# First attention of a two-layer perceiver: context channels split as 128 and 64 rows, and one PSUM set for keys and one for values

## What is computed

```python
xn = layernorm(x, ln_x_g, ln_x_b)            # x: context, 64 x 257 x 192
ln = layernorm(latents, ln_l_g, ln_l_b)      # 64 x 32 x 256
q = ln @ Wq.T
kv = jnp.concatenate([xn @ Wkv.T, ln @ Wlkv.T], axis=1)
k, v = (kv[..., :INNER], kv[..., INNER:])    # INNER 256 = 4 heads x 64
qn = rmsnorm(q, qn_g) * SCALE
kn = rmsnorm(k, kn_g)
attn = softmax(where(mask, qn @ kn.T, -max)) # 289 keys per head
out = (attn @ v) @ Wo.T + bo
```

## Time and profile before

| | |
|---|---|
| median of three executions | 3091.28 us (3088.22 to 3092.98) |
| the profiled execution's own time | 3089.94 us |
| its span in the trace | 3087.9 us |
| TensorE busy, share of the span | 85% |
| VectorE busy | 68% |
| ScalarE busy | 48% |
| GpSimd busy | 20% |

### The profile page before, as it was taken

How to read it: one execution, slowest core, us unless ns; L and a number is a source line. 1 busy time by engine, 2 the same in 40 slices (tenths; PEclk the granted TensorE clock), 3 DMA queues, 4 the chain that set the end, 5 groups by cost and what they waited for, 6 DMA issues and landing times. The chain is left out here.

```text
span 3087.9 us, 80338 instructions
## 1 busy us (share of the span) xinstructions
PE 2610.6 (85%) x29948; PEld 1986.1 (64%) x29949; DVE 2089.9 (68%) x5002; ACT 1473.9 (48%) x4043; POOL 619.5 (20%) x809
## 2 busy tenths in 40 slices
PE   6699998799789999999979999957467777779993
PEld 3488887355668888888857777743143333569993
DVE  6588887567458887877836777765379999632222
ACT  3555554355135555455516777722467665013330
POOL 3355553111000000000002222210222221012224
PEclk8899999899889999999999999979689999769996
DMA  3122221000400000000001111112000001351113
GB/s 94 49 65 62 66 66 30 34 1 0 171 2 2 3 3 2 3 3 3 2 18 34 31 31 33 31 31 109 7 1 1 1 1 55 113 219 36 36 37 92
DMA packets 69031, 121.90 MB, mean 39 GB/s; under 512 B 10176, under 2 KB 51360, under 8 KB 64224
## 3 DMA queue, kind: packets, MB, share of 16 engines
q1 hardware_dynamic: 65424, 109.70, 10.8%
q0 software_dynamic: 3408, 9.31, 1.1%
HBM read 99.12 MB, written 17.69 MB: 38 GB/s over the span
## 5 line engine op out<-in xcount | busy, mean ns | idle before, releaser
L1316 PE MATMUL s_ps<-s3e_xT,s_down 128*128 128x128 f32 x2048 | 263.1, 284 | 16.6 <-issue 16.6
L1316 PEld LDWEIGHTS s_ps<-s3e_xT,s_down 128*128 128x128 f32 x2048 | 251.0, 198 | 32.9 <-issue 27.3
L1327 PE MATMUL s_ps<-s_up,s3e_gh 128*128 128x256 f32 x1024 | 244.7, 384 | 3.1 <-DVE s3e_gh L1485 2.2
L1327 PEld LDWEIGHTS s_ps<-s_up,s3e_gh 128*128 128x128 f32 x1024 | 187.9, 193 | 26.0 <-DVE s3e_gh L1485 2.6
L1375 ACT ACTIVATE s3e_gh<-s_ps 128x512 f32<-128x512 f32 x128 | 76.6, 598 | 260.8 <-PE s_ps L1327 238.6
L1730 ACT ACTIVATE s4b_pr<-s4b_sc,s4b_nm 128x257 f32<-128x257 f32 x256 | 127.8, 503 | 109.1 <-DVE s4b_nm L1778 108.9
L2633 ACT ACTIVATE s6e_hT<-s_ps,s_b 128x128 f32<-128x128 f32 x312 | 84.9, 383 | 187.4 <-PE s_ps L2606 187.4
L2274 DVE SCALAR_TENSOR_TENSOR s5c_fresh<-s_ps,s5c_state 128x1024 f32<-128x1024 f32 x124 | 151.4, 1221 | 11.6 <-PE s_ps L2228 4.9
L1361 ACT ACTIVATE s3e_apart<-s3e_number,s3e_picksT 128x128 f32<-128x128 f32 x512 | 156.1, 388 | 1.6
L2657 DVE TENSOR_TENSOR s6e_y<-s_ps,s_b 128x256 f32<-128x256 f32 x39 | 16.6, 425 | 202.3 <-PE s_ps L2620 202.3
L2606 PEld LDWEIGHTS s_ps<-s6e_xT,s6e_w 128*128 128x128 f32 x1248 | 147.3, 194 | 5.4 <-ACT s6e_xT L2637 3.5
(11 more groups left out here) (429 smaller groups left out, 6398.4 us busy)
## 6 DMA issues: line engine op xcount, KB each, us to landing
s_w<-p_w SPq DMA_DIRECT2D x16, 1024.0 KB, 12.4
s4b_cT<-ctxT SPq DMA_DIRECT2D x64, 192.8 KB, 2.4
s1b_cx<-ctx SPq DMA_DIRECT2D x64, 192.0 KB, 2.7
s1b_cT<-ctxT SPq DMA_DIRECT2D x64, 192.0 KB, 2.9
s_results<-s6e_y SPq DMA_DIRECT2D x39, 128.0 KB
s_down<-p_down SPq DMA_DIRECT2D x1, 4096.0 KB, 21.9
s_up<-p_up SPq DMA_DIRECT2D x1, 4096.0 KB, 31.2
s_silu_z<-s5p_sz SPq DMA_DIRECT2D x4, 1024.0 KB, 4.5
```

Of the source, the lines that this page charges most:

```text
L1316: mm = pe.matmul(banks[:, H_BANK + i % 2, tok(e)], lhsT=down[:, k, i * CH + e, :], rhs=xT[:, c.u, k, :], start=k == 0, stop=k == KT - 1)
L1327: mm = pe.matmul(banks[:, Y_BANK, 0:D], lhsT=gh[:, o.u, e, :], rhs=up[:, e, :], start=e == 0, stop=e == NE - 1)
```

## The change

The 192 channels are laid out as 128 rows and a rest of 64. The rest is stored twice, on partitions 0 to 63 and again on 64 to 127, both of the context (`ctxR`, 128 partitions x 2 x 256 tokens per batch in place of 96 x 2 x 256) and of the weights. A projection is now one product with 128 rows for each token tile, then one with 64 rows for each, of which tile 0 uses the lower half of the array's rows and tile 1 the upper half. The two token tiles write to two different banks, so a batch takes both banks of its pair and nothing alternates any more: a projection waits for the reader of the batch just before (`kr_ready`, `vv_ready`). On VectorE the scaling of the values of `n` moves from the end of the step to behind L741, ahead of the key norm L744. The two ScalarE copies of the keys' transposes now each signal `kT_ready`, and each of the two score products waits for its own.

```diff
+CR = (slice(0, P), slice(0, P // 2))
...
-        wkv = sb("wkv", [DH, 2, 2 * D])
-        wc = sb("wc", [DH, 2, 2 * D])
+        wkv = sb("wkv", [P, 2, 2 * D])
+        wc = sb("wc", [P, 2, 2 * D])
...
-                    pe.matmul(banks[:, 6, :], lhsT=bc(cvec[:, 1, k:k + 1], DH, P), rhs=wkv[:, k, :], start=k == 0, stop=k == 1)
+                    pe.matmul(banks[:, 6, :], lhsT=bc(cvec[CR[k], 1, k:k + 1], CR[k].stop, P), rhs=wkv[CR[k], k, :], start=k == 0, stop=k == 1)
...
-        cT = sb("cT", [DH, U, 2, 2 * P])
+        cT = sb("cT", [P, U, 2, 2 * P])
...
-                sp.dma_start(cT[:, c.u, :, :], I["ctxT"][c.b, :, :, 0:2 * P]).then_inc(c_loaded[c.u], 16)
+                sp.dma_start(cT[:, c.u, :, :], I["ctxR"][c.b, :, :, 0:2 * P]).then_inc(c_loaded[c.u], 16)
...
+            def projected(c, bank, cols):
+                for j in range(2):
+                    pe.matmul(banks[:, bank + j, 0:D], lhsT=cT[:, c.u, 0, tok(j)], rhs=wc[:, 0, cols], start=True, stop=False)
+                for j in range(2):
+                    rows = slice(j * P // 2, (j + 1) * P // 2)
+                    mm = pe.matmul(banks[:, bank + j, 0:D], lhsT=cT[rows, c.u, 1, tok(j)], rhs=wc[rows, 1, cols], start=False, stop=True)
+                return mm
...
-                    pe.wait_ge(kT_ready, a.b + 1)
...
                     for k in range(KT):
+                        pe.wait_ge(kT_ready, KT * a.b + k + 1)
                         mm = pe.matmul(banks[:, S_BANK, 0:NK], lhsT=qb[:, a.u, k, :], rhs=kT[:, a.u, k, :], start=k == 0, stop=k == KT - 1)
...
-                    after(pe, kr_ready, c.b - 1)
-                    for j in range(2):
-                        for k in range(2):
-                            mm = pe.matmul(banks[:, K_BANK + c.u, j * D:(j + 1) * D], lhsT=cT[:, c.u, k, tok(j)], rhs=wc[:, k, 0:D], start=k == 0, stop=k == 1)
-                    mm.then_inc(keys, 1)
+                    after(pe, kr_ready, c.b)
+                    projected(c, K_BANK, slice(0, D)).then_inc(keys, 1)
...
-                    after(pe, vv_ready, c.b - 1)
-                    for j in range(2):
-                        for k in range(2):
-                            mm = pe.matmul(banks[:, V_BANK + c.u, j * D:(j + 1) * D], lhsT=cT[:, c.u, k, tok(j)], rhs=wc[:, k, D:2 * D], start=k == 0, stop=k == 1)
-                    mm.then_inc(values, 1)
+                    after(pe, vv_ready, c.b)
+                    projected(c, V_BANK, slice(D, 2 * D)).then_inc(values, 1)
...
-                        ins = act.activation(kT[:, n.u, k, 0:2 * P], banks[:, TR_BANK, 2 * k * P:2 * (k + 1) * P], ACT.Identity, scale=vec[:, 3, k:k + 1])
-                    ins.then_inc(kT_ready, 1)
+                        act.activation(kT[:, n.u, k, 0:2 * P], banks[:, TR_BANK, 2 * k * P:2 * (k + 1) * P], ACT.Identity, scale=vec[:, 3, k:k + 1]).then_inc(kT_ready, 1)
...
                     dve.tensor_reduce(nm[:, a.u, :], sc[:, a.u, :], AXX, ALU.min).then_inc(sc_ready, 1)
                 if n:
+                    dve.wait_ge(values, n.b + 1)
+                    if o:
+                        dve.wait_ge(pv, o.b + 1)
+                    scaled(vv, V_BANK, n, slice(D, 2 * D)).then_inc(vv_ready, 1)
                     dve.wait_ge(rn_ready, n.b + 1)
...
-                if n:
-                    dve.wait_ge(values, n.b + 1)
-                    if o:
-                        dve.wait_ge(pv, o.b + 1)
-                    scaled(vv, V_BANK, n, slice(D, 2 * D)).then_inc(vv_ready, 1)
...
+    split = lambda w: c(np.stack([w[:P], np.concatenate([w[P:], w[P:]])], axis=1))
...
+    r["ctxR"] = c(split(a["ctx_768"].transpose(2, 0, 1).reshape(192, -1)).reshape(P, 2, 64, 257).transpose(2, 0, 1, 3))
```

More of the change, by code:

```diff
@@ L296, in phase1 @@
         bo = sb("bo", [P, D])
-        cvec = sb("cvec", [DH, 2, 2])
+        cvec = sb("cvec", [P, 2, 2])
         headmask = sb("headmask", [P, KT, H])
@@ L328, in phase1 @@
             cn = sa("cn", [B, DC])
-            cT = sa("cT", [DH, 2, B])
+            cT = sa("cT", [P, 2, B])
             csq = sa("csq", [B, D])
@@ L397, in _ @@
                 for k in range(2):
-                    pe.matmul(banks[:, 6, :], lhsT=bc(cvec[:, 1, k:k + 1], DH, P), rhs=wkv[:, k, :], start=k == 0, stop=k == 1)
+                    pe.matmul(banks[:, 6, :], lhsT=bc(cvec[CR[k], 1, k:k + 1], CR[k].stop, P), rhs=wkv[CR[k], k, :], start=k == 0, stop=k == 1)
                 pe.wait_ge(wg_ready, 1)
                 for k in range(2):
-                    mm = pe.matmul(banks[0:DH, 7, :], lhsT=bc(half[0:DH, :], DH, DH), rhs=wc[:, k, :], start=k == 0, stop=k == 1)
+                    mm = pe.matmul(banks[:, 7, :], lhsT=bc(half[CR[k], :], CR[k].stop, P), rhs=wc[CR[k], k, :], start=k == 0, stop=k == 1)
                 mm.then_inc(w_summed, 1)
@@ L405, in _ @@
                 for k in range(2):
-                    mm = pe.transpose(ps[0:DH, 0, 0, k * B:(k + 1) * B], cn[:, k * DH:(k + 1) * DH], g.ident[0:B, 0:B])
+                    mm = pe.transpose(ps[CR[k], 0, 0, k * B:(k + 1) * B], cn[:, k * P:k * P + CR[k].stop], g.ident[0:B, 0:B])
                 mm.then_inc(c_tr, 1)
@@ L409, in _ @@
                 for k in range(2):
-                    mm = pe.matmul(ps[0:B, 0, 1, :], lhsT=cT[:, k, :], rhs=wkv[:, k, :], start=k == 0, stop=k == 1)
+                    mm = pe.matmul(ps[0:B, 0, 1, :], lhsT=cT[CR[k], k, :], rhs=wkv[CR[k], k, :], start=k == 0, stop=k == 1)
                 mm.then_inc(c_proj, 1)
@@ L447, in _ @@
                 for k in range(2):
-                    ins = act.activation(cT[:, k, :], ps[0:DH, 0, 0, k * B:(k + 1) * B], ACT.Identity,
-                                         bias=cvec[:, 1, k:k + 1], scale=cvec[:, 0, k:k + 1])
+                    ins = act.activation(cT[CR[k], k, :], ps[CR[k], 0, 0, k * B:(k + 1) * B], ACT.Identity,
+                                         bias=cvec[CR[k], 1, k:k + 1], scale=cvec[CR[k], 0, k:k + 1])
                 ins.then_inc(cT_ready, 1)
@@ L508, in _ @@
                 for k in range(2):
-                    ins = dve.scalar_tensor_tensor(wc[:, k, :], banks[0:DH, 7, :], 2.0 / DC, wc[:, k, :], ALU.mult, ALU.add)
+                    ins = dve.scalar_tensor_tensor(wc[:, k, :], banks[:, 7, :], 2.0 / DC, wc[:, k, :], ALU.mult, ALU.add)
                 link(ins)
@@ L666, in step @@
                     pe.wait_ge(c_loaded[c.u], 16 * (c.turn + 1))
-                    after(pe, kr_ready, c.b - 1)
-                    for j in range(2):
-                        for k in range(2):
-                            mm = pe.matmul(banks[:, K_BANK + c.u, j * D:(j + 1) * D], lhsT=cT[:, c.u, k, tok(j)], rhs=wc[:, k, 0:D], start=k == 0, stop=k == 1)
-                    mm.then_inc(keys, 1)
+                    after(pe, kr_ready, c.b)
+                    projected(c, K_BANK, slice(0, D)).then_inc(keys, 1)
                 if n:
                     pe.wait_ge(kn_ready, n.b + 1)
-                    after(pe, kT_ready, n.b)
+                    after(pe, kT_ready, KT * n.b)
                     for k in range(KT):
@@ L732, in scaled @@
                 for j in range(2):
-                    ins = dve.scalar_tensor_tensor(to[:, c.u, j, :], banks[:, bank + c.u, j * D:(j + 1) * D], crs[:, bass.ds(2 * c.b + j, 1)], bias[:, cols], ALU.mult, ALU.add)
+                    ins = dve.scalar_tensor_tensor(to[:, c.u, j, :], banks[:, bank + j, 0:D], crs[:, bass.ds(2 * c.b + j, 1)], bias[:, cols], ALU.mult, ALU.add)
                 return ins
@@ L2749, in layout @@
     r["p1_bo"], r["p4_bo"] = np.tile(a[p + "bo"], (P, 1)), np.tile(a["L1_xattn_bo"], (P, 1))
-    r["p1_cvec"] = c(np.stack([col(a[p + "ln_x_g"], 96), col(a[p + "ln_x_b"], 96)], axis=1))
+    r["p1_cvec"] = c(np.stack([split(a[p + n].reshape(192, 1))[:, :, 0] for n in ("ln_x_g", "ln_x_b")], axis=1))
     r["p1_wq"], r["p1_wlkv"], r["p1_wo"] = (kp(a[p + n].T) for n in ("Wq", "Wlkv", "Wo"))
-    r["p1_wkv"] = kp(a[p + "Wkv"].T, 96)
+    r["p1_wkv"] = split(a[p + "Wkv"].T)
     r["p2_w"] = kp(np.concatenate([a["L0_attn_Wq"], *(a["L0_attn_Wkv"].reshape(256, 16, 80)[:, :, lo:hi].reshape(256, -1)
```

## The result

The changed kernel takes 3112.85 us, the median of four executions (3111.31 to 3114.55), the kernel before 3091.01 us: a ratio of 1.0071, 95% interval 1.0054 to 1.0089. It is 21.8 us slower. The forecast was 12.1 us slower, with a range that ended at 3112.0. Of the executions behind the ratios in this document, one of e2_order_alone (3903.61 us) and one of the kernel before (6749.18 us) lie far above all others and are left out.

What follows compares the result with a forecast made beforehand. TensorE's issue bounds the kernel before; after, TensorE waits 0.34 us a step for VectorE's key norm. 3089.94 (profiled) + 10.8 (steps) + 1.3 (loads) = 3102.0, against the median 3103.4; range 3083.5 to 3112 us.

Steps and rivals of the forecast that it cites:

- TensorE's issue bounds the kernel before, the key norm stands 0.1 behind it: First stage: a step lasts what TensorE issues, 5.96 us; waiting for VectorE's key norm is only 0.1 us away.
- The projection, 1.65 for 1.73: Each key or value projection on TensorE: 0.86 + 0.09 + 0.65 + 0.05 = 1.65 us against 1.73, saving 0.08.
- halves one after another: Rival: 64-row halves on TensorE do not share time, 0.7 us more a step, 3135 us; chance 0.05.
- The chain, 3.67 + 2.47: Scores through VectorE's key norm to the transposes' weight load 3.67 us, then TensorE's work 2.47: 6.14 a step.
- The split kT_ready buys nothing: Separate signals for the two key copies: no gain, one more wait in TensorE's queue, priced at nothing.
- I carry this 0.12 unchanged: Stage average: a step is 0.12 us longer than its summed parts, and stays so after the change.
- ScalarE does not join the chain, by 0.2: Probability transposes need ScalarE's share at 5.63 us after the scores' start; TensorE comes at 5.81.
- 1.3 us at the start for larger loads: Uncovered first loads of context and weights: 1.3 us more, at most 3.3, at least nothing.
- The range: Whole time 3083.5 to 3112 us, the top from a chain 0.15 longer; serial halves left out.
- The one on the other side: Rival: TensorE stays the bound, key norm done by 3.33 us, each step saves 0.16, 3083 us; chance 0.12.
- Balance: Rival: the chain from scores to transposes is shorter by some 0.1 to 0.2, 3091 to 3097 us; chance 0.2.
- Free shape changes: Rival: changing TensorE's array shape costs nothing, each projection saves 0.43 us, 3082 us; chance 0.08.

Runs made afterwards that it cites:

- e2_order_alone: Kernel before with only VectorE's scaling of the values moved ahead of the key norm, 96-row groups and alternating banks kept; ratio to before 1.0061.
- e1: Changed kernel with one kT_ready signal for both key copies again and one wait before the scores; 3105.69 us, ratio to before 1.0048.
- e7: Changed kernel with VectorE's key norm ahead of the scaled values, and one kT_ready signal for both copies; ratio to before 0.9993.
- e3: Changed kernel with the 64-row rests of both token tiles on partitions 0 to 63, so they cannot run side by side; 3133.12 us, ratio to before 1.0135.
- e12: Changed kernel without TensorE's wait for kT_ready before the key transposes; ratio to before 1.0052.
- e9: Changed kernel with TensorE's two waits before the key transposes swapped, kT_ready first, then kn_ready; ratio to before 1.0054.
- e10: Changed kernel with key norm ahead of scaled values, one kT_ready signal and four-step hardware loops in this stage; ratio to before 0.9997.

## Why the prediction went wrong, point by point

- *TensorE's issue bounds the kernel before, the key norm stands 0.1 behind it*: right. With VectorE's order moved and nothing else, the norm is what TensorE waits for, and the stretch grows by 17.7 us.
- *The projection, 1.65 for 1.73*: right in each term. L645's four take 0.96 for 0.86 + 0.09, L648's four 0.63 for 0.65; halves one after another cost 0.43 more. The Trainium skill has a change of tiling mode drain the engine ("TensorEngine Tiling (Array Packing)", Key Properties); the 0.10 at the entry agrees with it. Only the gain in the whole was less than its 0.08 a step: 2.6 us of the stretch, 0.04 a step.
- *The chain, 3.67 + 2.47*: right to 0.02 where no second wait stands on it (scores to norm's end 3.61, then 2.47). As the forecast's deciding step this held: the cover that the scaled values lost is what made the kernel slower.
- *"The split kT_ready buys nothing ... It adds one wait to TensorE's queue"*: this is the step that failed. It buys nothing, but it costs 8.0 us of the stretch. I had priced the wait by when it would be met, not by the instructions that it takes. On a queue that has become the chain, a register instruction between the norm and the load costs 0.07 in every step, and all of the split's instructions together 0.14 at every loop end. With one signal the same kernel takes 3105.69 us (e1), inside the range.
- *"I carry this 0.12 unchanged"*: failed too, and for the same reason. Of these 0.24 in two steps the kernel after has 0.45: 0.35 in the pause (0.74 against 0.39) and 0.10 in the scores behind it. The split makes 0.14 of the difference of 0.21. The other 0.07 is there with one signal too. In both, the load of the probability transposes starts together with its product (303.54), and the branch behind it; in the kernel before the load ran 0.21 ahead of its product (307.14 and 307.35), and the branch 0.11 ahead. That this is its cause is read from the records, not tested. The sum for two steps was 12.52 and is 12.89: 0.15 for the second wait, 0.21 here, 0.01 for the rest.
- *ScalarE does not join the chain, by 0.2*: right, but the room is less. The share ends 0.13 before the load that needs it, and a load follows what releases it by 0.05: 0.08 is left.
- *1.3 us at the start for larger loads*: the first projection starts at 120.9 against 121.0; nothing.
- *The range*: its top came from a chain 0.15 a step longer and left no room for an edit at nothing to cost something. Two waits of such an edit, ahead of the scores and ahead of the key transposes, stood on the queue that the forecast itself had made the critical one.
- *Rivals*: the changed kernel is none of them. The one on the other side had its place right, VectorE between the scores and the key norm: where e7 takes the scaled values out of that stretch, every second step falls to 5.93, where the rival had 5.92. The others stop at 6.15, for GpSimd's power and the values' bank behind it, so the time ends level with the kernel before rather than at 3083. *Balance* needed a chain shorter by 0.1 to 0.2, and the chain was as long as forecast. Free shape changes and halves one after another are both excluded, by 0.96 + 0.63 and by e3.

## What to carry to other kernels

Work that stands in a queue where the engine would wait anyway is free; the same work moved to where something is awaited costs what is left of its length once the slack there is used up. Here 0.79 us of scaling ahead of a norm made that norm start 0.34 to 0.57 later after the scores (e2 against before) and the step 0.28 longer, and what the halves saved on TensorE did not pay for it. Look for the order of the queue first: the same instructions with the norm ahead of the scaling gave 19.5 us back. And once a queue is the chain, price every wait and register instruction on it, whether the wait is met or not.

## What the runs showed that was not expected

- A weight load carries one semaphore wait in all of these traces. A second one takes an instruction of its own, and if it is the awaited wait that moves there, the load starts 0.12 to 0.13 us after the releaser's end instead of 0.05 (e12 against the changed kernel); the order of the two in the source did not decide it (e9).
- The cost of a loop's end on TensorE is not fixed: a pause of 0.13 beyond the matmuls before, 0.35 in the changed kernel, 0.21 with one signal, and nothing with halves one after another, all with the same two-step body. In the records two things go with it: when the loop's branch starts (0.40 ahead of the last transposes' products where the pause is nothing, 0.11 ahead where it is 0.13, 0.03 behind where it is 0.35), and the time from the branch to the scores' load (0.57 to 0.61 with three instructions between, 0.66 to 0.71 with four). That these two decide it is a reading, not tested.
- Steps that alternate by the loop's parity need not come from the loop: e10 kept 5.93 and 6.15 with a body of four.
